# Attention in 32 written-out steps in place of a loop of three rounds and its ends

## What is computed

```python
def _L2_attn_ref(x, Wq, Wk, Wv, Wu, bu):
    q = (x @ Wq).reshape(b, t, h, k).transpose(0, 2, 1, 3) * scale
    kk = (x @ Wk).reshape(b, t, h, k).transpose(0, 2, 1, 3) * scale
    v = (x @ Wv).reshape(b, t, h, k).transpose(0, 2, 1, 3)
    attn = jax.nn.softmax(jnp.einsum('bhqk,bhsk->bhqs', q, kk), axis=-1)
    out = jnp.einsum('bhqs,bhsk->bhqk', attn, v)
    return out.transpose(0, 2, 1, 3).reshape(b, t, h * k) @ Wu + bu
```

## Time and profile before

| what | us |
|---|---|
| median of three executions | 419.47 |
| the profiled execution | 416.06 |
| its span, first to last instruction | 414.3 |
| PE busy in the span | 350.9 (85%) |
| DVE, ACT, POOL busy | 283.2, 217.5, 189.2 |

### The profile page before, as it was taken

How to read it: one execution, slowest core, us unless ns; L and a number is a source line. 1 busy time by engine, 2 the same in 40 slices (tenths; PEclk the granted TensorE clock), 3 DMA queues, 4 the chain that set the end, 5 groups by cost and what they waited for, 6 DMA issues and landing times.

```text
span 414.3 us, 6910 instructions
## 1 busy us (share of the span) xinstructions
PE 350.9 (85%) x2145; PEld 246.1 (59%) x2147; DVE 283.2 (68%) x689; ACT 217.5 (52%) x541; POOL 189.2 (46%) x186
## 2 busy tenths in 40 slices
PE   5666259999999999999769699877258999999996
PEld 1552156787888878887467244374147756666662
DVE  2767876788878878877493587579798545555441
ACT  0534258677677767778547435261315634444441
POOL 4120025545454545545315800122110299999994
PEclk9867559999999999999977789968556999999999
DMA  6916000000000000000000795000000576666521
GB/s 185 235 21 205 0 0 1 2 2 2 2 0 0 0 0 0 0 0 2 1 2 5 288 329 197 2 0 2 1 0 2 193 273 215 222 208 224 204 101 52
DMA packets 17002, 32.87 MB, mean 79 GB/s; under 512 B 6032, under 2 KB 9808, under 8 KB 16976
## 3 DMA queue, kind: packets, MB, share of 16 engines
q1 hardware_dynamic: 16976, 32.55, 23.9%
HBM read 31.83 MB, written 0.72 MB: 79 GB/s over the span
## 4 chain that ended last, share of the span: by engine, by line
PE 61%; DVE 19%; ACT 9%; issue 6%; DMA 3%; POOL 1%; SPq 0%; DVEq 0%; ACTq 0%; POOLq 0%
PE ps L1020 14%; PE ps L1028 7%; PE ps L857 6%; PE ps L884 5%; PE ps L868 5%; PE ps L976 4%; ACT va_vb L619 4%; DVE ln L1504 2%; DVE negmax L1574 2%; PE ps L968 2%; PE ps L807 2%; DMA pT<-gates_row 1%; PE ps L910 1%; PE ps L834 1%; PE ps L833 1%
## 5 line engine op out<-in xcount | busy, mean ns | idle before, releaser
L504 POOL TENSOR_TENSOR va_vb<-va_vb,rowinv 128x512 f32<-128x512 f32 x64 | 67.2, 1050 | 72.1 <-DVE rowinv L1581 72.1
L619 ACT ACTIVATE va_vb<-ps,negmax 128x256 f32<-128x256 f32 x128 | 59.5, 472 | 11.2 <-DVE negmax L1574 10.9
L1020 PE MATMUL ps<-XS,w3hl 128*128 128x512 f32 x256 | 63.4, 406 | 0.7 <-ACT gT L590 0.7
L733 ACT ACTIVATE wy<-ps 128x512 f32<-128x512 f32 x64 | 38.2, 598 | 45.6 <-PE ps L1020 45.6
L1020 PEld LDWEIGHTS ps<-XS,w3hl 128*128 128x128 f32 x256 | 48.6, 193 | 17.2 <-issue 4.9
L1574 DVE TENSOR_REDUCE negmax<-ps 128x2 f32<-128x512 f32 x64 | 44.0, 688 | 7.8 <-PE ps L857 5.6
L857 PE MATMUL ps<-keys_gates,xcur 128*128 128x256 f32 x256 | 47.4, 308 | 2.2 <-DVE keys_gates L1566 2.2
L857 PEld LDWEIGHTS ps<-keys_gates,xcur 128*128 128x128 f32 x256 | 35.1, 193 | 14.8 <-issue 11.5
L868 PE MATMUL ps<-consts,va_vb 128*128 128x128 f32 x256 | 39.5, 277 | 4.2 <-POOL va_vb L504 2.4
L462 POOL TENSOR_TENSOR xn<-T,lnc 128x512 f32<-128x512 f32 x4 | 4.2, 1042 | 74.0 <-DVE lnc L1512 74.0
L868 PEld LDWEIGHTS ps<-consts,va_vb 128*128 128x128 f32 x256 | 29.7, 147 | 9.8 <-POOL va_vb L504 4.8
(11 more groups left out here) (323 smaller groups left out, 727.9 us busy)
## 6 DMA issues: line engine op xcount, KB each, us to landing
pT<-gates_row SPq DMA_DIRECT2D x18, 512.0 KB, 4.8
vproj<-gates_row SPq DMA_DIRECT2D x16, 512.0 KB, 5.4
gate_row_keys<-gates_row SPq DMA_DIRECT2D x14, 512.0 KB, 4.9
early<-in_f_in SPq DMA_DIRECT2D x1, 2048.0 KB, 8.8
consts<-in_consts SPq DMA_DIRECT2D x1, 816.0 KB, 4.9
x<-in_x SPq DMA_DIRECT2D x1, 512.0 KB, 3.7
w2raw<-in_f_in SPq DMA_DIRECT2D x1, 512.0 KB, 3.5
out<-in_f_out SPq DMA_DIRECT2D x1, 512.0 KB
```

Source lines behind the costliest of these rows:

```text
L504: gp.tensor_tensor(prob[:, n % 4], prob[:, n % 4], rowinv[:, n % 4, :].unsqueeze(2).broadcast_to([P, U, N]), ALU.mult).then_inc(S("p_scale ...
L619: ins = act.activation(prob[:, n % 4, u, :], ps[:, 1 + n % 2, u * N:(u + 1) * N], ACT.Exp, bias=negmax[:, n % 4, u:u + 1], accum_out=rowsu ...
L733: act.activation(act_out[:, kk % 2, :], ps[:, 2 * (kk % 3), :], ACT.Silu).then_inc(S("f3_act"), 1)
L1020: mm = pe.matmul(ps[:, 2 * (kk % 3) + w, :], w3hl[:, s, e, w * HID:(w + 1) * HID], XS[:, c * CHUNK:(c + 1) * CHUNK], start=(s == 0), stop= ...
```

## The change

`attention_steps` is written out for all rounds: 4 + 4 x 8 = 36 calls per engine, 32 of them for the four rounds, and no `Fori`. `j` is a number everywhere, so every wait is for a constant. The buffer `nscoef`, the copy `newton_factors` and the two waits for it are gone; `newton_y` and `newton_z` read their factors where they lie in the constants. The order of the steps on every engine and the arithmetic stay.

```diff
-        nscoef = sb("nscoef", [P, PAIRS, 2])
...
         def upto(eng, name, j, a_round, more):
-            if isinstance(j, int) and j * a_round + more <= 0:
+            if j * a_round + more <= 0:
                 return
             eng.wait_ge(S(name), j * a_round + more)
...
-        def attention_steps(eng, step, in_loop=None):
+        def attention_steps(eng, step):
             for k in range(-2, 2):
                 step(0, k, lambda pair: pair >= 0)
-            with eng.Fori(0, J - 1) as j:
-                if in_loop:
-                    in_loop(j)
+            for j in range(J):
                 for k in range(2, 2 + PAIRS):
-                    step(j, k, lambda pair: True)
-            for k in range(2, 2 + PAIRS):
-                step(J - 1, k, lambda pair: pair < PAIRS)
+                    step(j, k, lambda pair: j < J - 1 or pair < PAIRS)
+
+        def newton_in(j, k):
+            return j < J - 1 and k >= 2
+
+        def newton_factor(j, s, which):
+            at = 2 * (j * PAIRS + s) + which
+            return con("newton")[:, at:at + 1]
...
             def newton_z(j, s):
-                gp.wait_ge(S("ns_factors"), j + 1)
                 upto(gp, "nsy_ready", j, PAIRS, s + 1)
-                gp.tensor_tensor(nsZ[:], con("fold"), nscoef[:, s, 1:2].broadcast_to([P, C]),
+                gp.tensor_tensor(nsZ[:], con("fold"), newton_factor(j, s, 1).broadcast_to([P, C]),
                                  ALU.mult).then_inc(S("nsz_ready"), 1)
...
-                dve.wait_ge(S("ln_low"), 1 if isinstance(j, int) else 4)
+                dve.wait_ge(S("ln_low"), 1 if j + m // 2 == 0 else 4)
...
-            def newton_factors(j):
-                dve.tensor_copy(nscoef[:].rearrange("p s a -> p (s a)").unsqueeze(1),
-                                con("newton").rearrange("p (j n) -> p j n", j=J - 1)[:, bass.ds(j, 1), :]
-                                ).then_inc(S("ns_factors"), 1)
-                dve.wait_ge(S("ns_factors"), j + 1)
-
             def newton_y(j, s):
                 upto(dve, "nsz_ready", j, PAIRS, s + 1)
                 upto(dve, "ns_ax", j, PAIRS, s + 1)
-                stt(nsY[:], ps[:, 6, 0:C].unsqueeze(1).broadcast_to([P, 2, C]), nscoef[:, s, 0:1],
+                stt(nsY[:], ps[:, 6, 0:C].unsqueeze(1).broadcast_to([P, 2, C]), newton_factor(j, s, 0),
                     nsZ[:].unsqueeze(1).broadcast_to([P, 2, C]), ALU.mult, ALU.add).then_inc(S("nsy_ready"), 1)
...
-            attention_steps(dve, attention_step, in_loop=newton_factors)
+            attention_steps(dve, attention_step)
```

More of the change, by code:

```diff
@@ L508, in newton_z @@
             def newton_z(j, s):
-                gp.wait_ge(S("ns_factors"), j + 1)
                 upto(gp, "nsy_ready", j, PAIRS, s + 1)
-                gp.tensor_tensor(nsZ[:], con("fold"), nscoef[:, s, 1:2].broadcast_to([P, C]),
+                gp.tensor_tensor(nsZ[:], con("fold"), newton_factor(j, s, 1).broadcast_to([P, C]),
                                  ALU.mult).then_inc(S("nsz_ready"), 1)
             def step(j, k, there):
-                if not isinstance(j, int):
+                if newton_in(j, k):
                     newton_z(j, k - 2)
@@ L913, in step @@
             def step(j, k, there):
-                in_loop = not isinstance(j, int)
+                in_loop = newton_in(j, k)
                 if there(k + 1):
@@ L1554, in tokens @@
                 upto(dve, "scores_ready", j, 2 * PAIRS, 8 * m - 8)
-                dve.wait_ge(S("ln_low"), 1 if isinstance(j, int) else 4)
+                dve.wait_ge(S("ln_low"), 1 if j + m // 2 == 0 else 4)
                 src = XS[:].bitcast(F32).rearrange("p (j u g n) -> p j u g n", j=J, u=U, g=G)
-                at = j + m // 2
-                at = slice(at, at + 1) if isinstance(at, int) else bass.ds(at, 1)
+                at = slice(j + m // 2, j + m // 2 + 1)
                 dve.tensor_copy(xcur[:, m % 2, :].rearrange("p (u n) -> p u n", u=U).unsqueeze(1),
@@ L1586, in add_out @@
                 upto(dve, "out_turned", j, G, G + m + 1)
-                at = slice(j, j + 1) if isinstance(j, int) else bass.ds(j, 1)
+                at = slice(j, j + 1)
                 t = T[:].rearrange("p (j u g) c -> p j u g c", j=J, u=U)[:, at, :, m % 2, :]
```

## The result

Twenty executions of the changed kernel took a median of 414.60 us (412.87 to 419.39), twenty of the kernel before 418.75 us (415.55 to 422.34). The ratio is 0.9925, 95% interval 0.9898 to 0.9953: faster, by 0.75%. Two later measurements of the same two kernels gave 0.9886 (0.985 to 0.9921) and 0.9939 (0.9902 to 0.9975). The ratios leave out the executions over 1.5% longer than the fastest of their kernel, which count as a slower state of the chip, and so they are not the quotients of the medians. The forecast was 417.4 us, 0.9951 of 419.47.

What follows compares the result with a forecast made beforehand. PE was taken to bound the loop, so only its standing time counts; 1.64 us from jumps plus 0.45 us from register work gave 2.1 us off the 419.47 us median: 417.4 us, range 415.6 to 419.2.

Steps and rivals of the forecast that it cites:

- The jumps: Two jumps between loop rounds: steps 2 and 3 should become like steps 6 and 7, saving 2 x 0.82 = 1.64 us.
- The rival that the jump is not the price: At the jump `nsY` stays late, or the clock takes the gain back: 0.1 us saved or 419.3 us total; chance 0.14.
- The register work: Inside the rounds, DVE's register operations before the odd head's maxima: 0.09 us in five steps, 0.45 us saved.
- The rival that PE's own register operations cost 2.9 us: Throughout the rounds, PE's register operations delay its own stream: 5.0 us saved in all, 414.5 us; chance 0.10.
- The entry: Step 2 of round 1, 4.99 us long: taken as 0 gain, with ends 0 and 0.75 us.
- The factors in place: `newton_y` and `newton_z` read as many values from another tile: price 0, at most 0.6 us either way.
- The code: Rounds 2 and 3 become new text to fetch, hidden behind work fetched before: price 0.
- The third rival: Instruction fetch for rounds 2 and 3 is not hidden: PE stands 8 us if none is, 425.4 us; chance 0.06.
- The sum: Whole kernel: 1.64 + 0.45 = 2.1 us saved, all of it within the attention.
- Behind the attention: Work after the attention is unchanged and starts earlier by what is won; TensorE's clock may add 0.8 us either way.

## Why the prediction was right, and where its sizes were off

*The jumps.* Forecast 1.64 us, from making steps 2 and 3 like 6 and 7. Step 2 lost 0.64 us and step 3 0.29 at each of the two jumps; without the register work's 0.09 in step 2 that is 0.84 a jump, 1.68. Right. Which part of the jump has the price (branch, copy or the copy's wait) the prediction left open. The loop without the copy and the straight text with it show that it is the copy at that place: 1.51 us of the 2.16 go with it, and 0 with it in straight text. The rival that the jump is not the price falls: step 2 behind it lost its wait for `nsY`.

*The register work.* Forecast 0.45 us, 0.09 in five steps. Step 6 lost 0.09 in all three rounds. Behind the jumps step 2 took 4.24 us in the loop without the copy and 4.15 in straight text, the same again. Right, and shown apart by the version with one round written out. By what the prediction worked out from the section Sequencer and Instruction Queues of the Trainium skill's page Advanced Engine Details and Errata, it would have been nothing; the trace decides for 0.08 to 0.09 us in a step where the chain meets PE. The rival that PE's own register operations cost 2.9 us falls: steps 4, 5, 8 and 9 kept their length to 0.02 us.

*The entry.* Forecast 0, measured 4.99 us before and after. Right, and for the reason given: with `nsZ` moved on POOL it fell to 4.37.

*The factors in place.* Forecast 0. The version that reads the copy has the same 157.40 us.

*The code.* Forecast 0, with 6 more blocks in queue 8. The page of the profile shows 17 in place of 13, so 4 more, and in round 2 two blocks on each instruction queue without any hole in PE's loads. Transfers of the changed kernel in round 2:

```profile
q8 instruction: 2, 0.03, 0.4%
q14 instruction: 2, 0.02, 0.1%
```

The third rival falls: the rounds that fetch are as short as any.

*The sum.* 2.1 us forecast for the attention, 2.16 measured.

*Behind the attention* stands the term that was mis-sized: "what follows starts earlier by what is won", with 0.8 us either way for the clock. The measured medians lie 4.15, 3.2 and 1.4 us apart, and the ratios show 0.6 to 1.1% in place of 0.5%. The first median, 414.60 us, lies below the range's lower end of 415.6, the two later ones, 416.12 and 417.56, within the range. What follows started earlier and met the clock's changes otherwise: 21 of 44 executions in place of 11 of 84 had a high mean clock, and an execution with it is 3 to 5 us shorter. The version with the wait of 2.1 us, which has the same text in the attention and no execution with a high clock, speaks for the start and against the text as the reason. An earlier start is not always the better one: with `nsZ` moved it came 0.83 us earlier still, and 2 of 12 were high. I had taken the clock as noise of both signs around the median; it has two outcomes, some 4.6 us apart for the changed kernel (413.62 and 418.25), and the change moved their shares. Which way a shift moves them I could not have read from one profile. So the attention's 2.16 us were understood beforehand, and that the clock added to them and did not take from them was luck.

## What to carry to other kernels

Measure what a loop's end costs by its steps, first round against later ones and the steps behind the jump against their like inside the round; then look at what instruction stands behind the jump, for moving a small register-addressed copy from there may give most of what writing the loop out gives. A saving of a few microseconds ahead of stretches in which TensorE's clock falls is not passed on one for one: compare the changed stage by itself, and look at the clock's shares over many executions before believing the total. Where PE stands just ahead of a block of matmuls, work that nobody reads may hold the clock and be worth more than the edit; that was seen here at one place, in six executions.

## What was not expected of the hardware

The first DVE copy behind the loop's jump took 0.73 to 0.78 us and the same copy without a jump 0.15 to 0.18; the maxima in the same place behind a jump took their usual 0.69. What in the copy waits there (its address comes from the loop's register) is not settled. And 0.83 us less in the attention left the total no shorter (415.62 us) while nine idle matmuls more ahead of a later stage brought it to 414.37.
